# Second attention: the output projection's bias as a product of a row of ones on the matmul engine, in place of Pool's addition to the residual

## The chip, the cores and the metric

The kernel runs on one core of a Trainium2 chip. The metric is the device time of one execution in microseconds (us), and lower is better. The engines have short names here as in the profile: PE is TensorE (matrix products; PEld is its weight load), DVE is VectorE, ACT is ScalarE, POOL (or Pool) is GpSimd, SP is SyncE, which only issues DMAs. Each runs its own instruction stream; they meet at semaphores.

## The reference, cut to what matters

Eight sequences of 256 tokens, 256 features wide, go through a small tower:

```python
h = tok(x)                                   # smoothing over time, projection
h = h + attn0(layernorm(h))                  # causal softmax attention, 16 heads
h = h + moe(layernorm(h))                    # 8 experts, 2 chosen for each token
h = h + attn1(layernorm(h))                  # second attention, below
h = h + fp8_linear(layernorm(h))

# attn1, for x = its own layer norm of the input:
q, k, v = x @ Wq.T + bq, x @ Wk.T + bk, x @ Wv.T + bv      # 16 heads of 16
s = q @ k.T / 4
s = sigmoid(s - mu) * exp(s);  s = s / s.sum(-1)
out = (s @ v) @ Wo.T + bo
```

The change concerns `bo` in the last line, a vector of 256 that is added to every token's row.

## The kernel before, in words

The order of the work on each engine is written out by hand; no scheduler moves anything. The second attention is a loop over the eight batches (one sequence of 256 tokens each), called step b = 0 to 7 here. Every engine has its own `iteration(b, ...)`, and within one step the engines work on three batches at once: step b makes the scores of batch b, the projections of batch b+1, and the back end (division, output projection, residual sum, moments) of batch b-1.

PE's order in step b (the last nested functions of the kernel): the first scores `pass1(0)` to `pass1(7)`, two heads each, into two alternating PSUM areas, with other work between them: the turned input of batch b+1, the last two groups of value products of batch b-1 (`weigh_values`), `project_rows` for q and k of batch b+1 (L2045), the turns of batch b-1's result, and the output projection of batch b-1 as two token tiles, `project_token_tile(misc[0], n_oT, 3, 0)` before `pass1(7)` and `(..., 3, 1)` after it (L2051). The second tile raises `n_wo`. Then come `pass2(0)`, the value projection of batch b+1 (L2051 again), `pass2(1)` to `pass2(7)` with fillers (`idle_product`, L2081) among them, and the first two groups of value products of batch b (L2074). The scores are L2060. `pass1` and `pass2` make the same scores twice, because ACT turns one copy into exp (L845) and the other into a sigmoid (L846), changing its function table once in each step. A score pass p waits until ACT has emptied its area, pass p-2.

DVE's order in step b: division of batch b-1's result (L1550, L1558), the parts of q and k of batch b+1 (L1335, L1342), `sum_h3(b-1)` (L1568: `h` = projected rows in PSUM + `h`), its moments, `biased_v(b+1)` (L1376), then eight multiplications of the exp part by the sigmoid part (L1346), which the value products of PE wait for, two multiplications each.

Pool's order in an iteration: `gather(b+2)` (four indirect DMAs that fetch the experts' rows, L703), `biased_h(b)` (L712: h = h + bo1, both token tiles in one 128x512 instruction), two small norm steps (L690, L692), and the second bfloat16 part of q and of k for batch b+1 (L718). Pool runs ahead of PE: its iteration 0 starts before PE's step 0 has ended its first scores, and from iteration 2 on its gather and `biased_h` stand in the time of PE's step b-1.

SP copies the q and k parts into the stacked layout that the scores read (L568, twelve DMAs for each batch). `pass1(0)` of the next step waits for them to land.

`bo1` is loaded once, spread over all 128 partitions; `ones_row` is a [1, 128] row of ones that Pool fills at the start and that nothing reads. The last batch's back end stands behind the loop: two token tiles into two banks (L2308), then for each the sum with `h` (L1673) and its moments on DVE.

Of the kernel before, what the change touches and what calls it, by code (L numbers as in the profile page):

```python
# [28 lines left out]
ALU = mybir.AluOpType  # L29
# [3 lines left out]
P = 128  # L33
B, C_IN, T = 8, 128, 256
D, HEADS = 256, 16
DH = D // HEADS
QT = T // P
TILES = B * QT
TOKENS = TILES * P
DC = D // P  # L40
# [38 lines left out]
def stages(batch, first, last):  # L79

    return not isinstance(batch, int) or first <= batch <= last
# [17 lines left out]
def tower_kernel(nc, a, out):  # L99
    with ExitStack() as ctx:  # L100
        def sb(name, shape, dt):
            return ctx.enter_context(nc.sbuf_tensor(name, shape, dt))

        def sem(name):
            return ctx.enter_context(nc.semaphore(name))


        h = sb("h", [P, TILES, D], F32)
# [6 lines left out]
        w1T = sb("w1T", [P, 4, DC, D], F32)  # L115
# [5 lines left out]
        bo1 = sb("bo1", [P, D], F32)  # L121
# [3 lines left out]
        ones_row = sb("ones_row", [1, P], F32)  # L125
# [52 lines left out]
        def carve(shape, dt, size):  # L178
            n = size
            for s in shape:  # L180
                n *= s
            start = used[0]
            used[0] = start + (n + 31) // 32 * 32
            assert used[0] <= ARENA, used[0]
            v = arena[:, start:start + n].bitcast(dt)
            if len(shape) == 2:
                v = v.rearrange("p (a b) -> p a b", a=shape[0])
            if len(shape) == 3:
                v = v.rearrange("p (a b c) -> p a b c", a=shape[0], b=shape[1])
            if len(shape) == 4:  # L190
                v = v.rearrange("p (a b c d) -> p a b c d", a=shape[0], b=shape[1], c=shape[2])
            return v
# [52 lines left out]
        n_xh = carve([QT, D], F32, 4)  # L245
# [21 lines left out]
        n_oT = w0T[:, TOPK + 1]  # L267
# [34 lines left out]
        last_rows_bank = [misc[0], psum[:, 3, :]]  # L302
# [39 lines left out]
        S = {n: sem(n) for n in names}  # L342
# [3 lines left out]
        LAST = B - 1  # L346
# [115 lines left out]
        with nc.Block() as block:  # L462
# [158 lines left out]
            def _(pool):  # L621
# [38 lines left out]
                def iteration(b, u, k):  # L660
                    if stages(b - 1, 0, LAST):

                        if isinstance(b, int) and b == 1:
                            pool.wait_ge(S["w_in"], LATE_LOADS)
                        pool.wait_ge(S["xh_done"], QT * b)
                        v = h[:, bass.ds((b - 1) * QT, QT), :]
                        pool.tensor_tensor(v, v, bo0[:].rearrange("p (o d) -> p o d", o=1).to_broadcast([P, QT, D]),
                                           ALU.add).then_inc(S["hbo_done"], 1)
                    if stages(b - 1, 0, LAST):
                        norm_scale(b - 1, 1, S["mv2"], S["veps2"], S["rstd2"])  # L670
                    if stages(b + 2, 0, LAST):
                        norm_scale(b + 2, 0, S["mv1"], S["veps1"], S["rstd1"])
                    if stages(b - 2, 0, LAST):

                        pool.wait_ge(S["xslot_done"], b)
                        settled(pool)
                        for c in range(TOPK):
                            for q in range(QT):
                                pool.indirect_dma_start(  # L679
                                    out=xg, out_offset=bass.IndirectOffsetOnAxis(ap=xslot[:, c, q:q + 1], axis=0),  # L680
                                    in_=x2h[:, u, q, :], in_offset=None).then_inc(scat[u], 16)

                batches(pool, iteration, B + 2)

                def scale1(b, n, got, s_eps, s_rstd):
                    pool.wait_ge(got, QT * (b + 1))
                    settled(pool)

                    scale, shift = (1.0 + LN1_EPS, LN_EPS * LN1_EPS) if n == 0 else (1.0, LN_EPS)
                    pool.tensor_scalar(n_veps[:, n, :], n_mom[:, n, :, 1], scale, shift, ALU.mult, ALU.add).then_inc(s_eps, 1)  # L690
                    pool.wait_ge(s_eps, b + 1)
                    pool.tensor_tensor(n_rs[:, n, :], n_veps[:, n, :], half_exp[:], ALU.pow).then_inc(s_rstd, 1)  # L692

                def gather(b):

                    done = min(EARLY_TILES + 2 * EXPERTS, MOE_TILES) if b == 0 else min(2 * EXPERTS * (b + 1), MOE_TILES)
                    pool.wait_ge(S["place_step"], PLACE_STEPS)
                    for u in range(2):
                        pool.wait_ge(y_st[u], 16 * ((done + 1 - u) // 2))
                    wait(pool, S["comb_done"], 4 * b)  # L700
                    for c in range(TOPK):
                        for q in range(QT):
                            pool.indirect_dma_start(  # L703
                                out=n_y[:, c, q, :], out_offset=None, in_=yg[0:done * P, :],
                                in_offset=bass.IndirectOffsetOnAxis(ap=pos[:, c, b * QT + q:b * QT + q + 1], axis=0)
                            ).then_inc(y_in[b % 2], 16)

                def biased_h(b):

                    pool.wait_ge(S["n_xh"], QT * (b + 1))  # L710
                    v = h[:, bass.ds(b * QT, QT), :]
                    pool.tensor_tensor(v, v, bo1[:].rearrange("p (o d) -> p o d", o=1).to_broadcast([P, QT, D]),  # L712
                                       ALU.add).then_inc(S["n_hbo"], 1)

                def second_part(b, which, got, done):

                    pool.wait_ge(got, b + 1)
                    pool.tensor_copy(n_qkp[which][:, 1], n_qkr[which]).then_inc(done, 1)  # L718

                def iteration(b, u, k):  # L720
                    if stages(b + 2, 3, LAST):
                        gather(b + 2)
                    if stages(b, 0, LAST):
                        biased_h(b)
                    if stages(b - 2, 0, LAST):
                        scale1(b - 2, 1, S["m_mv"], S["m_eps"], S["m_rstd"])
                    if stages(b + 2, 3, LAST):
                        scale1(b + 2, 0, S["n_mv"], S["n_eps"], S["n_rstd"])
                    if stages(b + 1, 1, LAST):
                        second_part(b + 1, 0, S["n_qr"], S["n_qm"])  # L730
                        second_part(b + 1, 1, S["n_kr"], S["n_km"])
                    if b == 0:
                        scale1(2, 0, S["n_mv"], S["n_eps"], S["n_rstd"])

                for b in range(2):
                    gather(b)
                    scale1(b, 0, S["n_mv"], S["n_eps"], S["n_rstd"])
                gather(2)
                all_batches(iteration)

            @block.scalar
# [272 lines left out]
            def _(dve):  # L1014
# [548 lines left out]
                def sum_h3(b):  # L1563

                    dve.wait_ge(S["n_wo"], b + 1)
                    dve.wait_ge(S["n_hbo"], b + 1)
                    hv = h[:, bass.ds(b * QT, QT), :]
                    dve.tensor_tensor(hv, misc[0].rearrange("p (q d) -> p q d", q=QT), hv, ALU.add).then_inc(S["n_h3"], 1)  # L1568

# [95 lines left out]
                for q in range(QT):  # L1665
                    divided_slots(q, EARLY_SLOTS, HEADS, o1_last).then_inc(S["n_on"], 1)
                maximum(LAST - 1)
                dve.wait_ge(S["n_hbo"], B)
                dve.wait_ge(S["x3_done"], QT * LAST)
                for q in range(QT):  # L1670
                    n = LAST * QT + q
# [69 lines left out]
            def _(pe):  # L1741
# [3 lines left out]
                for j in range(DC):  # L1745
                    mm = pe.transpose(misc[0][:, j * P:(j + 1) * P], wraw[:, 8, j, 0:P], ident[:])
# [302 lines left out]
                def project_token_tile(bank, x, w, q):  # L2049
                    for c in range(DC):  # L2050
                        mm = pe.matmul(bank[:, q * D:(q + 1) * D], x[:, c, q * P:(q + 1) * P], w1T[:, w, c, :],  # L2051
                                       start=(c == 0), stop=(c == DC - 1))
                    return mm

                def scores(b, u, p, done):
# [214 lines left out]
                def kept_busy(n):  # L2270

                    for _ in range(n):
                        pe.matmul(misc[1].rearrange("p (c t) -> p c t", c=DC), identb[:], fqT[:], start=True, stop=True)
# [25 lines left out]
                for q in range(QT):  # L2299
                    pe.wait_ge(S["n_on"], QT * LAST + q + 1)  # L2300
                    for c in range(DC):
                        mm = pe.transpose(last_rows_bank[q][:, c * P:(c + 1) * P], n_onat[:, q, c * P:(c + 1) * P], ident[:])
                    mm.then_inc(S["n_ot2"], 1)
                kept_busy(1)
                for q in range(QT):
                    pe.wait_ge(S["n_oT"], B + q)
                    for c in range(DC):
                        mm = pe.matmul(last_rows_bank[q][:, 0:D], n_oT[:, c, q * P:(q + 1) * P], w1T[:, 3, c, :],  # L2308
                                       start=(c == 0), stop=(c == DC - 1))
                    mm.then_inc(S["n_wo"], 1)  # L2310
                kept_busy(8)

                pe.wait_ge(S["q_step"], 1)
# [66 lines left out]
```

## Time and profile before

| | |
|---|---|
| time, median of 3 runs | 770.08 us (767.87 to 770.21) |
| profiled execution, its own time | 775.55 us |
| its span, first to last instruction | 773.7 us |
| PE busy / DVE / ACT / POOL, share of the span | 91% / 57% / 45% / 19% |
| second attention, step 0 to the last batch's back end | about 544 us to 742 us |
| start of `pass1(0)` on PE, steps 1 to 7 | 566.4, 592.0, 615.7, 639.9, 663.8, 686.4, 709.2 us |

Times inside the profile count from the first instruction. The chain of waits is the work that ended last, followed back: each piece is what the next one waited for. "issue" in it is time in which nothing that the profile shows was waited for. An entry such as `[0.49 <-DVE arena L1346]` at the end of a row says how long the engine stood idle before it and what ended that. A float32 matmul of this kernel appears as two records, so the two matmuls of one token tile read x4. `arena` is one large buffer that holds most tiles, and `psum` all accumulators.

### The profile page before, as it was taken

The numbers are of one execution on the slowest core, as the hardware profiler recorded it, in microseconds if no ns is written. First come the engines' busy times: TensorE is split into PE (matmuls) and PEld (weight loads), VectorE is DVE, ScalarE is ACT, GpSimd is POOL, SyncE is SP. The second block draws the span as 40 slices with busy tenths as digits, with TensorE's granted clock in tenths as the row PEclk, the third lists the DMA queues.
The fourth block names the chain that finished last, engine by engine and source line by source line (L and its number), as shares of the span: only waits on it lengthen the run. The fifth ranks groups of instructions, "written<-read, shape, count | busy, mean of one in ns | idle before, by whom it ended". The sixth has DMA issues, their size and how long they took to land.

```text
span 773.7 us, 16147 instructions
## 1 busy us (share of the span) xinstructions
PE 701.8 (91%) x5671; PEld 576.0 (74%) x5681; DVE 444.4 (57%) x1129; ACT 350.6 (45%) x599; POOL 147.4 (19%) x180
## 2 busy tenths in 40 slices
PE   5697999999889999999999999999889999999855
PEld 4476777777767998999999999998556666665533
DVE  3567587778763542244322232233479988977686
ACT  2242453355335221212211212131779898899735
POOL 2010112331322021000000100200465553411000
PEclk9799999999998999999999999999999999999975
DMA  6979264466374566555555555574555774555002
GB/s 166 201 138 271 41 91 89 76 89 89 76 171 159 183 195 239 196 184 197 161 187 198 188 187 198 173 184 115 93 88 73 110 107 67 81 63 69 1 14 96
DMA packets 70839, 102.54 MB, mean 133 GB/s; under 512 B 8416, under 2 KB 58600, under 8 KB 70640
## 3 DMA queue, kind: packets, MB, share of 16 engines
q1 hardware_dynamic: 67376, 93.15, 50.4%
q0 software_dynamic: 3136, 8.40, 4.3%
q8 instruction: 43, 0.70, 0.4%
q14 instruction: 28, 0.23, 0.1%
q10 hardware_dynamic: 256, 0.07, 0.0%
HBM read 63.75 MB, written 12.58 MB: 99 GB/s over the span
## 4 chain that ended last, share of the span: by engine, by line
PE 65%; DVE 12%; DMA 8%; issue 5%; ACT 4%; POOL 2%; SPq 2%; ACTq 0%; DVEq 0%; POOLq 0%
PE psum L2102 18%; PE psum L2153 17%; DMA arena<-arena 7%; PE psum L2060 3%; PE psum L1782 3%; PE psum L2045 3%; PE psum L2074 3%; DVE arena L1346 2%; DVE arena L1199 2%; PE psum L1806 2%; POOL w0T L703 2%; PE psum L2051 1%; SPq L568 1%; PE psum L1811 1%; PE psum L2130 1%
## 5 line engine op out<-in xcount | busy, mean ns | idle before, releaser
L2102 PEld LDWEIGHTS psum<-arena 128*128 128x128 f32 x1248 | 144.9, 192 | 3.3 <-issue 1.7
L2102 PE MATMUL psum<-arena 128*128 128x128 f32 x1248 | 146.1, 275 | 1.2 <-issue 1.1
L2153 PE MATMUL psum<-arena 128*128 x624 | 141.3, 380 | 0.8 <-DVE arena L1492 0.8
L875 ACT ACTIVATE arena<-psum,arena 128x128 f32<-128x128 f32 x156 | 44.5, 368 | 190.1 <-PE psum L2102 106.6
L2153 PEld LDWEIGHTS psum<-arena 128*128 128x128 f32 x624 | 115.6, 190 | 15.3 <-issue 1.2
L1474 DVE TENSOR_SCALAR arena<-psum,arena 128x128 f32<-128x128 f32 x156 | 44.0, 344 | 81.0 <-PE psum L2102 64.8
L2060 PE MATMUL psum<-arena 96*128 96x256 bf16 x512 | 74.8, 276 | 8.4 <-ACT arena L845 4.2
L1346 DVE TENSOR_TENSOR arena<-arena 128x1024 f32<-128x1024 f32 x64 | 77.9, 1284 | 1.3 <-ACT arena L845 1.3
L1199 DVE TENSOR_REDUCE arena<-psum 128x6 f32<-128x768 f32 x64 | 59.3, 954 | 28.9 <-PE psum L1811 27.5
L703 POOL DMA_INDIRECT w0T<-yg,pos x32 | 40.3, 1260 | 185.6 <-DMA yg<-arena 177.4
L2060 PEld LDWEIGHTS psum<-arena 96*128 96x128 bf16 x512 | 44.8, 98 | 40.5 <-issue 14.7
L1492 DVE TENSOR_TENSOR arena<-psum,arena 128x256 f32<-128x256 f32 x39 | 16.6, 424 | 97.0 <-PE psum L2153 97.0
L846 ACT ACTIVATE arena<-psum,neg_mu 128x1024 f32<-128x1024 f32 x64 | 67.9, 1120 | 5.9 <-PE psum L2060 5.6
L845 ACT ACTIVATE arena<-psum 128x1024 f32<-128x1024 f32 x64 | 62.1, 1034 | 15.5 <-DVE arena L1492 7.9
L817 ACT ACTIVATE arena<-psum 128x768 f32<-128x768 f32 x64 | 48.5, 808 | 21.7 <-PE psum L1828 21.3
L1806 PE MATMUL psum<-arena 96*128 96x256 bf16 x128 | 36.8, 288 | 11.1 <-DMA arena<-arena 5.9
L679 POOL DMA_INDIRECT xg<-arena,xslot x32 | 31.5, 985 | 53.9 <-DVE xslot L1118 46.6
L1823 PE MATMUL psum<-arena 97*128 97x256 bf16 x128 | 35.9, 281 | 4.7 <-DMA arena<-arena 4.0
L656 POOL TENSOR_SCALAR veps<-mv 128x2 f32<-128x2 f32 x16 | 5.4, 339 | 173.7 <-DVE mv L1054 173.7
L2074 PE MATMUL psum<-arena 128*32 128x256 f32 x512 | 34.3, 385 | 2.6 <-DVE arena L1346 1.4
L690 POOL TENSOR_SCALAR arena<-arena 128x2 f32<-128x2 f32 x16 | 6.5, 405 | 143.0 <-DVE arena L1329 125.3
L1790 PE MATMUL psum<-w0T,arena 128*128 128x256 f32 x128 | 31.7, 401 | 2.2 <-DVE arena L1040 1.7
(309 smaller groups left out, 1201.4 us busy)
## 6 DMA issues: line engine op xcount, KB each, us to landing
arena<-in_L_ffn_w_dram SPq DMA_DIRECT2D x47, 1024.0 KB
arena<-arena SPq DMA_DIRECT2D x192, 128.0 KB, 4.6
arena<-xg SPq DMA_DIRECT2D x39, 128.0 KB
yg<-arena SPq DMA_DIRECT2D x39, 128.0 KB, 1.7
out_dram<-arena SPq DMA_DIRECT2D x8, 256.0 KB, 2.1
xg<-zeros SPq DMA_DIRECT2D x9, 128.0 KB, 2.6
arena<-in_x_dram SPq DMA_DIRECT2D x8, 128.0 KB, 3.2
arena<-in_L_ffn_b_dram SPq DMA_DIRECT2D x1, 1024.0 KB
```

The costliest lines, as they stand in the source:

```text
L703: pool.indirect_dma_start(out=n_y[:, c, q, :], out_offset=None, in_=yg[0:done * P, :], in_offset=bass.IndirectOffsetOnAxis(ap=pos[:, c, b ...
L817: act.activation(probs[:, p], area[p % 2][:, :, 0:3 * P], ACT.Exp).then_inc(S["exp_done"], 1)
L845: return act.activation(out, in_, ACT.Exp)
L846: return act.activation(out, in_, ACT.Sigmoid, bias=neg_mu[:])
L875: ins = act.activation(hidT[:, v, c, :], psum[:, 2 * v, c * P:(c + 1) * P], ACT.Relu, bias=b1c[:, v, c:c + 1])
L1199: dve.tensor_reduce(mx[:, 2 * p:2 * p + 2, :], area[p % 2][:, :, 0:3 * P].rearrange("p i (n k) -> p i n k", k=P), AX, ALU.max).then_inc(S[ ...
L1346: dve.tensor_tensor(first[:, u, p], first[:, u, p], second[:, p % 4], ALU.mult).then_inc(S["prodD"], 1)
L1806: pe.matmul(dst[:, 0:T], stackq[0:ROWS, u, hd, P:T], stackk[0:ROWS, u, hd, :], start=True, stop=False)
L2060: mm = pe.matmul(area[p % 2][:, i, kt * T:(kt + 1) * T], stackk1[u][0:ROWS, hd, kt * P:(kt + 1) * P], stackq1[u][0:ROWS, hd, :], start=Tru ...
L2074: mm = pe.matmul(pv_out[32 * i:32 * i + 32, g], n_vaug[:, u, kt, head_of(4 * g + i), :], first[:, u, 2 * g + i // 2, i % 2, kt * T:(kt + 1 ...
L2102: mm = pe.matmul(psum[:, 2 * v + c // HALF, (c % HALF) * P:(c % HALF + 1) * P], w1b[:, i % W1_BUFS, d, c * P:(c + 1) * P], xtT[:, v, d, :] ...
L2153: mm = pe.matmul(y_bank, hidT[:, u, c, :], w2s[:, one(e), c, :].rearrange("p o n -> p (o n)"), start=(c == 0), stop=(c == HC - 1))
```

## The change: what it does

Pool's `biased_h` goes, with its wait for `n_xh` and with DVE's two kinds of waits for `n_hbo` (in `sum_h3` and in the last batch). On PE each token tile of the output projection gets a third product into the same accumulator: `ones_row` as the stationary operand (one row, 128 columns), `bo1[0:1]` as the moving one (one row, 256 columns), both float32. There are 16 such products, two for each batch. Nothing else is edited; the other operands, buffers and waits stay.

```diff
-                def biased_h(b):
-
-                    pool.wait_ge(S["n_xh"], QT * (b + 1))
-                    v = h[:, bass.ds(b * QT, QT), :]
-                    pool.tensor_tensor(v, v, bo1[:].rearrange("p (o d) -> p o d", o=1).to_broadcast([P, QT, D]),
-                                       ALU.add).then_inc(S["n_hbo"], 1)
...
-                    if stages(b, 0, LAST):
-                        biased_h(b)
...
                 def sum_h3(b):
                     dve.wait_ge(S["n_wo"], b + 1)
-                    dve.wait_ge(S["n_hbo"], b + 1)
...
                 maximum(LAST - 1)
-                dve.wait_ge(S["n_hbo"], B)
...
                 def project_token_tile(bank, x, w, q):
                     for c in range(DC):
                         mm = pe.matmul(bank[:, q * D:(q + 1) * D], x[:, c, q * P:(q + 1) * P], w1T[:, w, c, :],
-                                       start=(c == 0), stop=(c == DC - 1))
+                                       start=(c == 0), stop=(c == DC - 1 and w != 3))
+                    if w == 3:
+                        mm = pe.matmul(bank[:, q * D:(q + 1) * D], ones_row[:], bo1[0:1, :], start=False, stop=True)
                     return mm
...
-                        mm = pe.matmul(last_rows_bank[q][:, 0:D], n_oT[:, c, q * P:(q + 1) * P], w1T[:, 3, c, :],
-                                       start=(c == 0), stop=(c == DC - 1))
-                    mm.then_inc(S["n_wo"], 1)
+                        pe.matmul(last_rows_bank[q][:, 0:D], n_oT[:, c, q * P:(q + 1) * P], w1T[:, 3, c, :],
+                                  start=(c == 0), stop=False)
+                    pe.matmul(last_rows_bank[q][:, 0:D], ones_row[:], bo1[0:1, :], start=False, stop=True
+                              ).then_inc(S["n_wo"], 1)
```

PE in step 1, around the output projection, before (the scores are L2060, the two token tiles `w1T,w0T`, the value projection `w1T,arena`):

```order
L2060 MATMUL psum<-arena 128x256 x8
L2051 MATMUL psum<-w1T,w0T 128x256 x2
L2060 MATMUL psum<-arena 128x256 x4
L2051 MATMUL psum<-w1T,w0T 128x256 x2
L2060 MATMUL psum<-arena 128x256 x4
L2051 MATMUL psum<-w1T,arena 128x256 x4
L2060 MATMUL psum<-arena 128x256 x8
```

The same place of PE after the change, where the lines have moved up by 9 to 11:

```order
L2051 MATMUL psum<-arena 128x256 x8
L2040 MATMUL psum<-w1T,w0T 128x256 x2
L2043 MATMUL psum<-bo,ones_row 128x256
L2051 MATMUL psum<-arena 128x256 x4
L2040 MATMUL psum<-w1T,w0T 128x256 x2
L2043 MATMUL psum<-bo,ones_row 128x256
L2051 MATMUL psum<-arena 128x256 x4
L2040 MATMUL psum<-w1T,arena 128x256 x4
L2051 MATMUL psum<-arena 128x256 x8
```

One product stands ahead of the last first-pass scores and one ahead of the first second-pass scores; the value projection and all later passes stand behind both.

Pool at the start of the loop, before (gather of batch 2, addition for batch 0, parts of q and k of batch 1, norm steps, gather of batch 3, addition for batch 1):

```order
L703 DMA w0T<-yg,pos 128x256 x4
L712 TENSOR_TENSOR h<-h,bo 128x512
L718 CAST arena<-arena 128x512 x2
L690 TENSOR_SCALAR arena<-arena 128x2
L692 TENSOR_TENSOR arena<-arena,half_exp 128x2
L703 DMA w0T<-yg,pos 128x256 x4
L712 TENSOR_TENSOR h<-h,bo 128x512
L690 TENSOR_SCALAR arena<-arena 128x2
```

The same place of Pool after the change:

```order
L703 DMA w0T<-yg,pos 128x256 x4
L711 CAST arena<-arena 128x512 x2
L690 TENSOR_SCALAR arena<-arena 128x2
L692 TENSOR_TENSOR arena<-arena,half_exp 128x2
L703 DMA w0T<-yg,pos 128x256 x4
L690 TENSOR_SCALAR arena<-arena 128x2
```

The parts of q and k now follow the gather directly in iteration 0; from iteration 1 on the norm steps do.

## Rows read from the trace of the kernel before

**Rows 1.** Chain of waits in step 4: start, length, what ran.

```profile
650.74 1.13 PE psum L2051 x4
651.87 0.44 PE psum L2060 x4
652.31 0.86 PE psum L2051 x4
...
653.62 1.74 PE psum L2051 x8
...
656.07 5.63 DVE arena L1346 x4
...
662.91 0.85 issue
```

**Rows 2.** Token tiles of the output projection: ns min/median/max, weight load and matmul.

```profile
L2051 PEld LDWEIGHTS psum<-w1T,w0T x56: 186/190/193, 579.8 to 720.2; 128*128 128x128 f32 x56
L2051 PE MATMUL psum<-w1T,w0T x56: 377/379/484, 579.8 to 720.4; 128*128 128x256 f32 x56
```

**Rows 3.** Pool's eight additions, in the same columns.

```profile
L712 POOL TENSOR_TENSOR h<-h,bo x8: 1265/1370/1432, 551.8 to 698.3; 128x512 f32<-128x512 f32 x8
```

**Rows 4.** Timeline of DVE: the eight multiplications of steps 4 and 6.

```profile
655.99 10.24 DVE L1346 TENSOR_TENSOR arena<-arena 128x1024 f32<-128x1024 f32 x8
...
702.53 9.16 DVE L1346 TENSOR_TENSOR arena<-arena 128x1024 f32<-128x1024 f32 x8
```

**Rows 5.** Timeline of Pool beside the multiplications of step 4.

```profile
658.04 1.43 POOL L712 TENSOR_TENSOR h<-h,bo 128x512 f32<-128x512 f32 x1
```

**Rows 6.** Timeline of DVE in step 0: the rest of q.

```profile
551.32 0.88 DVE L1335 SCALAR_TENSOR_TENSOR arena<-psum,cols,arena 128x256 f32<-128x256 f32 x2 [6.15 <-ACT arena L853]
```

**Rows 7.** Chain of waits from step 0 to step 1.

```profile
551.83 1.28 POOL h L712
553.10 0.56 POOL arena L718
...
564.92 5.67 POOL w0T L703
...
573.63 1.68 DVE h L1356 x4
```

**Rows 8.** Timeline of PE: groups of steps 1 to 4 with idle time ahead.

```profile
578.49 0.63 PE L2039 MATMUL psum<-ident,w0T 128*128 128x128 f32 x4 [2.54 <-DVE arena L1335]
...
590.99 1.07 PE L2074 MATMUL psum<-arena 128*32 128x256 f32 x16 [0.49 <-DVE arena L1346]
...
614.07 1.07 PE L2074 MATMUL psum<-arena 128*32 128x256 f32 x16 [0.22 <-DVE arena L1346]
615.69 0.60 PE L2060 MATMUL psum<-arena 96*128 96x256 bf16 x4 [0.55 <-issue]
...
639.92 0.60 PE L2060 MATMUL psum<-arena 96*128 96x256 bf16 x4 [1.13 <-issue]
...
663.76 0.60 PE L2060 MATMUL psum<-arena 96*128 96x256 bf16 x4 [0.85 <-issue]
```

**Rows 9.** Timeline of the weight loads: ahead of step 3's first scores.

```profile
615.66 0.35 PEld L2060 LDWEIGHTS psum<-arena 96*128 96x128 bf16 x4 [1.01 <-DMA arena<-arena]
```

**Rows 10.** Chain of waits: ends of steps 5 and 6, step 7, behind the loop.

```profile
686.29 0.08 issue
...
709.09 0.09 issue
...
719.99 0.16 issue
...
737.82 1.14 PE psum L2308 x4
```

**Rows 11.** Timeline of DVE: the last batch's two sums.

```profile
739.10 0.42 DVE L1673 TENSOR_TENSOR h<-psum,h 128x256 f32<-128x256 f32 x1 [1.43 <-PE psum L2308]
...
740.12 0.39 DVE L1673 TENSOR_TENSOR h<-psum,h 128x256 f32<-128x256 f32 x1
```

## The prediction

> **What bounds the kernel now.** I read the page's busy shares first, then the chain of waits over the second attention, then each engine's timeline at the places the change touches. The shares say that Pool is idle four fifths of the time and PE almost never, so the change moves work from the idlest engine to the busiest; whether that costs anything is read from the waits of each step.
>
> In steps 1 to 6 the chain runs through the very place that is edited: first token tile, scores, second tile, scores, value projection, all on PE, then DVE's multiplications, then PE's value products and the next step's first scores [rows 1]. Two things in that chain matter. PE still idles ahead of the value products or of the next first scores in steps 1 to 4 [rows 8]: in step 1 for DVE's multiplications (0.49 us), in step 2 for them (0.22) and then for the stacked q and k to land (0.55), in steps 3 and 4 mainly for the landing (1.13 and 0.85). That it is the landing is told by the weight load there, whose wait a DMA ended [rows 9]. That DMA path starts at the q and k projections, which stand ahead of the token tiles in PE's order, so a longer token tile does not delay it. Steps 5 and 6, where nothing is gathered any more, leave PE only 0.08 and 0.09 us at that point [rows 10].
>
> **The change part by part.**
>
> *Added: 16 products on PE.* A token tile's four records take 0.86 us in the chain, the value projection's eight take 1.74 [rows 1], so one record costs 0.217 us and one float32 product with 256 columns, two records, 0.435; a batch's pair costs 0.87. The new product has the same columns and type, but one row in place of 128; no row of this trace has that. From below, four bfloat16 score products with as many columns take 0.44 [rows 1], 0.11 each; from above, a tile that follows a wait takes 1.13 [rows 1], 0.565 per product. I take 0.435, the row with the same type and columns.
>
> The weight load of a record, 0.19 us [rows 2], lies beside the record before it: four records of 0.379 us, each with its own load, leave 0.86 in the chain [rows 1], so loads add nothing to the term. The Trainium skill, "TensorE: Matmul & The Clock Gate", Part 3 ("The mechanism"), says the contrary for a case like this: a weight load overlaps running products only when it goes to another row group. Full-height tiles here do hide their loads, so the trace disagrees for them; no run here shows it for a one-row operand behind a full one. By that rule the sum below would be +7.7 us; it is the fourth rival.
>
> Where the pair lands: the last first-pass scores come 0.435 later, all second-pass scores but the first 0.87, and with them ACT, which works from what PE gives it. The value projection ends 0.87 later, so the multiplications begin 0.87 later. The cost of a step is 0.87 less the idle time of PE before the next first scores: step 1: 0.87 - 0.49 = 0.38; step 2: 0.87 - 0.22 - 0.55 = 0.10; step 3: none, 1.13 covers it; step 4: 0.87 - 0.85 = 0.02; step 5: 0.87 - 0.08 = 0.79; step 6: 0.87 - 0.09 = 0.78 [rows 8, 10]. In step 7 no values are projected, and what counts is when ACT gets its last first-pass scores, one product late: 0.435 - 0.16 of slack [rows 10] = 0.28. Behind the loop both tiles are on the path: the first ends at 737.82 + 1.14 = 738.96 [rows 10], its sum starts 0.14 later; the second would be ready at 738.96 + 0.87 + 0.14 = 739.97, while its sum starts at 740.12 [rows 11]. With 0.87 more it is 740.84: 0.72 late. Together 3.07 us.
>
> *Removed: eight additions on Pool, 1.37 us each* [rows 3]. Pool's time is worth nothing in itself; two effects are. First, in steps 1 to 4 an addition runs beside the multiplications [rows 5], and the eight of step 4 take 10.24 us against 9.16 in step 6, where no addition is beside them [rows 4]: 1.08 us, and it falls on one of the first four, which take 5.63 [rows 1]. When the additions go, the multiplications start 0.87 late and the fourth ends 0.21 early. So this buys no time by itself: it keeps DVE from holding up the value products, and the idle time above can absorb PE's delay. Between no relief and all of it, I take all; with none, step 1 would lose all 0.87 and step 2 0.87 - 0.55 = 0.32, 0.7 us more.
>
> Second, in step 0 one addition is on the chain: Pool does it before the second part of q [rows 7]. The rest of q is ready at 551.32 + 0.88 = 552.20 [rows 6]; the copy follows the addition at 553.10 [rows 7]. It can start about 0.1 us after 552.20, so 0.8 earlier. Behind it on Pool stand k's part, the norm steps and the next gather; all of that is the chain down to the sum at 573.63 [rows 7] and PE's turn at 578.49, ahead of which PE idles 2.54 us [rows 8]. So the 0.8 arrives: -0.8. The other additions (start of step 1, steps 5 and 6) have no one waiting behind them.
>
> *Waits.* None is added. DVE's wait for the addition goes, but the addition was done long before the projected rows it is summed with. The next thing late is always PE.
>
> *The sum:* +3.07 - 0.8 = +2.27 us. The profiled execution took 775.55 us (span 773.7 and 1.85 around it), so 777.8 under the profiler; it stands 5.5 us above the median of the runs, and I carry the difference over to that median: 770.08 + 2.27 = 772.35. With the bounds of the product, by the same subtraction: at 0.11, steps 1 to 4 and 7 lose nothing, 5 and 6 lose 0.14 and 0.13, the end 0.07, so 0.34 - 0.8 = -0.5 us; at 0.565, 0.64 + 0.36 + 0 + 0.28 + 1.05 + 1.04 + 0.41 + 0.98 - 0.8 = +4.0 us.
>
> **The rivals.**
>
> *Clearly slower: the landing is no cover.* The runs are 5.5 us shorter than the profiled execution; if part of this is that the stacks land earlier there, steps 2 to 4 wait only for DVE (0.22 in step 2 [rows 8], taken for all three) and lose 0.65 each, 1.95 in place of 0.12: +4.1 us, 774.2. For it speaks that the cover is thin (0.55 and 0.85 against 0.87); against it that 1.01 us of a weight load's wait is a DMA's [rows 9], and DMA time is the least likely to shrink unprofiled. It decides from the point at which the landing comes 0.5 us earlier.
>
> *No change: the long descriptor run goes.* One indirect DMA in step 0 takes 5.67 us on Pool [rows 7], beside five multiplications back to back. If the shifted phases let it through earlier, step 0 gains as much as PE idles behind it, 2.54 [rows 8], not 0.8: +0.5 us, 770.6. Against it: Pool and DVE move together there, so their phases stay.
>
> *Slightly faster: one-row products are nearly free*, at the lower bound: -0.5 us, 769.6. Nothing in the rows speaks for it but the bfloat16 pace.
>
> *Much slower: each record of a product exposes its weight load*, 0.19 us [rows 2]: 0.815 for a product, 1.63 for a pair. Step by step 1.14 + 0.86 + 0.50 + 0.78 + 1.55 + 1.54 + 0.66 + 1.48 - 0.8 = +7.7 us, 777.8. The hidden loads of the full tiles speak against it [rows 1, 2]. It is what the rule of the Trainium skill quoted above would do here.
>
> **How the numbers follow.** Main case 0.50; no cover 0.27; long run gone 0.13; nearly free 0.06; exposed loads 0.04. A measurement of this kernel tells about 0.3% from no change, 2.3 us. The main case, 772.4 with its own range 771.2 to 773.4, sits on that line: 0.24 of its 0.50 is within, 0.25 above, 0.01 below. No cover and exposed loads are slower (0.30, and 0.01 within); the long run gone is within (0.12, and 0.01 below); nearly free is within for 0.04, below for 0.02. That makes faster 0.04, same 0.41, slower 0.55. The range 769.7 to 775.2 holds the main case, no cover with a microsecond above it and the long run gone; left out are the exposed loads and half of the nearly free case, and the runs' own scatter.
>
> **What would show it.** Right: two new records per product, 0.21 to 0.22 us apart; token tiles of 1.3 us in the chain; no addition on Pool and every set of eight multiplications near 9.2 us; step 0's copy of q's part at about 552.25 on the same clock; the first scores of steps 1 to 7 moved by about -0.8, -0.4, -0.3, -0.3, -0.3, +0.5 and +1.3 us; the last batch's second sum 0.7 late against its first tile's start. Wrong: if steps 3 to 5 grow too, the landing was no cover; if the total moves by less than 1 us, step 0 gave more than its 0.8; if multiplications still show a long one, something else of Pool holds DVE up.

## The result, and the profile after

The changed kernel took 776.09 us (median of 6 runs, 774.64 to 777.96) against 769.35 us for the kernel before beside it (6 runs, 766.81 to 770.21): ratio 1.0072 (95% interval [1.0043, 1.0101]), or 5.5 us; the medians alone stand 6.7 us apart. Twelve later runs gave 776.64 us against 771.22 us, 1.0077 [1.0044, 1.0110], or 5.9 us (medians 5.4 us apart). Ratios, here and below, are of the fast runs alone and leave out two slow ones, 1019.66 us with the additions moved and 791.77 us with two products. So it is slower, as forecast, but by more than twice the 2.27 us of the sum, and above the range.

The two profiled spans, 773.7 and 776.1 us, differ by only 2.4 us. That is because in the profile after, the first scores of step 0 stand at 539.50 us, before at 543.79, and nothing ahead of step 0 was edited. From there to the end it is 229.95 us before and 236.64 after, 6.7 us longer. The loop has therefore to be read step by step. The table has the time from each step's first scores to the next (step 7: to the end of the span), from the PE timelines. A star marks a step in which the granted clock fell below 0.75 for some 3 to 4 us ahead of the last batch's back end. The last 27 to 30 us of every one of these kernels run at 0.50 and carry no star: from the last batch's second sum to the end each takes 33.6 to 33.7 us.

| kernel | steps 0+1 | 2 | 3 | 4 | 5 | 6 | 7 and behind |
|---|---|---|---|---|---|---|---|
| before | 48.20 | 23.70 | 24.23 | 23.84 | 22.61 | 22.81 | 64.56* |
| changed | 49.53* | 24.11 | 24.37 | 24.10 | 23.81 | 24.12 | 66.60* |
| changed, repeated | 49.76* | 24.12 | 24.39 | 24.31 | 23.81 | 24.11 | 65.00 |
| 128 rows (full height) | 49.23* | 23.63 | 24.49 | 23.51 | 23.22 | 23.52 | 64.11 |
| 96 rows | 48.88* | 23.51 | 24.43 | 23.63 | 23.21 | 23.51 | 64.09 |
| 64 rows | 49.83* | 24.10 | 24.17 | 24.58 | 23.81 | 24.11 | 65.00 |
| 32 rows | 48.20 | 24.11 | 24.14 | 24.23 | 23.81 | 24.11 | 65.01 |
| neither product nor addition | 46.90 | 23.49 | 24.14 | 23.88 | 22.58 | 22.73 | 64.51* |
| two products | 49.11 | 24.97 | 24.84 | 25.33 | 24.68 | 24.96 | 66.62 |
| products and additions | 49.94 | 24.65 | 24.66 | 24.66 | 23.95 | 24.11 | 66.29* |
| additions moved, no product | 47.40 | 23.34 | 24.16 | 23.66 | 22.52 | 22.63 | 64.57* |

Steps 5 and 6 repeat to 0.01 us between the two profiles of the changed kernel and those with 32 and 64 rows. They are what the causes are read from.

The chain of waits of the kernel after, in step 5, through both token tiles (start, length, what ran; the scores are L2051 now, the tiles and the value projection L2040, the new product L2043). It is the place of [rows 1] one step later:

```profile
672.45 1.13 PE psum L2040 x4
673.58 0.62 PE psum L2043 x2
674.20 0.54 PE psum L2051 x4
674.75 0.86 PE psum L2040 x4
675.61 0.62 PE psum L2043 x2
676.24 0.54 PE psum L2051 x4
676.78 1.73 PE psum L2040 x8
```

The tile keeps its 0.86 us. The product's two records take 0.62 us, not 0.435, and the four scores behind it 0.54, not the 0.44 of [rows 1]. A product thus lengthens the chain by 0.62 + 0.10 = 0.72 us, a pair by 1.44. Each start stands 0.31 or 0.32 us behind the one ahead of it at three places (first record, second record, next scores), where a tile's records stand 0.22 apart.

The timeline of the weight loads shows what is held up, at the first of these two products:

```profile
673.51 0.29 PEld L2043 LDWEIGHTS psum<-bo,ones_row 1*128 1x128 f32 x2 [0.33 <-issue]
674.13 0.33 PEld L2051 LDWEIGHTS psum<-arena 96*128 96x128 bf16 x4 [0.33 <-issue]
```

The load unit idles 0.33 us ahead of the product's loads and again ahead of the scores' loads. The first load starts only 0.31 us behind the start of the tile's last record, so the product can't start earlier. It is so at all 16 products of this trace.

The new line by itself (ns min/median/max, weight load and matmul):

```profile
L2043 PEld LDWEIGHTS psum<-bo,ones_row x28: 181/182/184, 577.1 to 723.5; 1*128 1x128 f32 x28
L2043 PE MATMUL psum<-bo,ones_row x28: 374/426/478, 577.1 to 723.7; 1*128 1x256 f32 x28
```

The weight load is even a little shorter than the tiles' 190 ns [rows 2]; it comes late, it isn't longer. Half of the matmul records last 478 ns instead of 374: the first of each product.

DVE's multiplications in the kernel after, in step 4 and step 5, the rows that answer to [rows 4], and all 64 together:

```profile
655.04 9.16 DVE L1337 TENSOR_TENSOR arena<-arena 128x1024 f32<-128x1024 f32 x8
679.15 9.16 DVE L1337 TENSOR_TENSOR arena<-arena 128x1024 f32<-128x1024 f32 x8
...
L1337 DVE TENSOR_TENSOR arena<-arena x64: 1215/1219/1226, 556.2 to 734.0; 128x1024 f32<-128x1024 f32 x64
```

Step 4's set took 10.24 us before; now none of the 64 is longer than 1.226 us, where the longest was 2.300.

Step 0 in the kernel after, first DVE's rest of q, then Pool (rows that answer to [rows 6, 7]):

```profile
548.32 0.88 DVE L1326 SCALAR_TENSOR_TENSOR arena<-psum,cols,arena 128x256 f32<-128x256 f32 x2 [7.44 <-ACT arena L844]
```

```profile
546.59 0.95 POOL L703 DMA_INDIRECT w0T<-yg,pos  x1 [0.30 <-issue]
549.27 0.61 POOL L711 CAST arena<-arena 128x512 bf16<-128x512 f32 x1 [1.74 <-DVE arena L1326]
...
561.15 5.67 POOL L703 DMA_INDIRECT w0T<-yg,pos  x1 [0.30 <-issue]
```

The copy of q's part begins 0.07 us after the rest of q is done (548.32 + 0.88 = 549.20). Before, it began 0.90 us after (552.20 to 553.10). The indirect DMA of 5.67 us is still there, unchanged.

PE's idle time in the kernel after, ahead of step 4's first scores and inside step 4, which answers to [rows 8]:

```profile
637.51 0.60 PE L2051 MATMUL psum<-arena 96*128 96x256 bf16 x4 [0.49 <-DMA arena<-arena]
656.04 0.61 PE L2051 MATMUL psum<-arena 96*128 96x256 bf16 x4 [0.34 <-ACT arena L837]
```

Of the 1.13 us of waiting for the stacked q and k, 0.49 is left. Ahead of the value products PE no longer waits for DVE in steps 1 to 6.

Behind the loop, the chain of the kernel after (tiles L2299, products L2301, sum L1662), which answers to [rows 10, 11]:

```profile
738.97 1.13 PE psum L2299 x4
740.10 0.62 PE psum L2301 x2
740.73 1.06 PE psum L2299 x4
741.79 0.64 PE psum L2301 x2
742.43 0.02 issue
742.45 0.43 DVE h L1662
```

From the first tile's start to the second sum's start it is 3.48 us, where it was 740.12 - 737.82 = 2.30 [rows 10, 11]: 1.18 us more, not 0.72.

Last, what disturbs a comparison of single steps. Stretches of the kernel after around step 0: length, busy time (and count) of PE, PEld, DVE, ACT and Pool, granted clock, DMA share, GB/s:

```profile
540.00:543.00 3.00, 1.63 (x13) 1.17 (x12) 0.88 (x3) 1.96 (x3) 0.28 (x1) 1.00 0.13 44
543.00:547.00 4.00, 3.85 (x12) 2.77 (x13) 0.00 (x0) 2.83 (x5) 3.08 (x4) 0.57 0.25 69
547.00:550.00 3.00, 3.00 (x20) 2.48 (x19) 0.96 (x3) 2.21 (x5) 1.14 (x2) 1.00 0.43 116
```

The granted clock falls from 1.00 (2.4 GHz) towards the lower level (1.2 GHz; the mean of the 4 us is 0.57) after a stretch in which PE was busy 1.63 of 3 us, and returns. Step 0 lost by it what its own gain was worth and more. The kernel before has such a fall in step 7, the kernel after a second one there.

### The profile page after: what moved, and what is told of

It is laid out like the page before. It is cut to its first block, busy times and chain, and to the rows that moved or that the text cites. A ratio compares the mean times of both kernels' runs of the same rounds, so it can differ in the third digit from the quotient of the medians.

```text
span 776.1 us, 16206 instructions
## 1 busy us (share of the span) xinstructions
PE 713.6 (92%) x5713; PEld 580.8 (75%) x5713; DVE 438.4 (56%) x1129; ACT 351.5 (45%) x599; POOL 134.2 (17%) x172
## 4 chain that ended last, share of the span: by engine, by line
PE 72%; DVE 10%; DMA 7%; issue 5%; ACT 4%; POOL 1%; SPq 1%; ACTq 0%; DVEq 0%; POOLq 0%
PE psum L2093 18%; PE psum L2144 17%; DMA arena<-arena 5%; PE psum L2051 5%; PE psum L2034 3%; PE psum L2065 3%; PE psum L1771 3%; PE psum L2040 3%; DVE arena L1190 2%; PE psum L1795 2%; PE psum L1779 1%; PE psum L2121 1%; PE psum L1800 1%; PE psum L1833 1%; POOL w0T L703 1%
## 5 line engine op out<-in xcount | busy, mean ns | idle before, releaser
L2051 PE MATMUL psum<-arena 96*128 96x256 bf16 x512 | 73.8, 277 | 6.9 <-ACT arena L836 3.5
L2051 PEld LDWEIGHTS psum<-arena 96*128 96x128 bf16 x512 | 44.5, 98 | 39.2 <-issue 12.6
L1337 DVE TENSOR_TENSOR arena<-arena 128x1024 f32<-128x1024 f32 x64 | 73.4, 1219 | 0.0
L703 POOL DMA_INDIRECT w0T<-yg,pos x32 | 37.9, 1186 | 184.9 <-DMA yg<-arena 176.5
```

Source lines behind the costliest of these rows:

```text
L703: pool.indirect_dma_start(out=n_y[:, c, q, :], out_offset=None, in_=yg[0:done * P, :], in_offset=bass.IndirectOffsetOnAxis(ap=pos[:, c, b ...
L1337: dve.tensor_tensor(first[:, u, p], first[:, u, p], second[:, p % 4], ALU.mult).then_inc(S["prodD"], 1)
L2051: mm = pe.matmul(area[p % 2][:, i, kt * T:(kt + 1) * T], stackk1[u][0:ROWS, hd, kt * P:(kt + 1) * P], stackq1[u][0:ROWS, hd, :], start=Tru ...
```

## The experiments

The first question was why a pair of products costs 1.44 us. The theory: the change of height (the rows, that is partitions, of the operands), from 128 rows to one and back, leaves weight loads uncovered. The rival: any added product costs this much there. The second question was what Pool's additions had cost.

**Full height.** The product takes the identity and the bias spread over 128 partitions, which gives the same sum.

```diff
-    ... ones_row[:], bo1[0:1, :], start=False, stop=True
+    ... ident[:], bo1[:], start=False, stop=True
```

> The bias product with full-height operands: the 128x128 identity as stationary, the bias row spread over 128 partitions as moving operand; same columns, same place. Theory A (the one-row product is slow because it differs in height from its neighbours: it takes 0.63 us in the changed kernel's chain where the neighbours' pace gives 0.435, its weight load not being hidden): each product goes back to 0.43-0.44, steps 5 and 6 lose 0.8 us each in place of 1.2, the whole gains about 16 x 0.19 less what idle time covers = 2 to 3 us on the changed kernel, so 772 to 774 us, a ratio of about 1.004 to 1.006 to the kernel before. Theory B (the height does not matter; the loss is from somewhere else, such as the slow clock in step 0): same time as the changed kernel, ratio about 1.007, and a product still takes 0.63.

Measured: 775.06 us against 771.73, ratio 1.0034 [1.0008, 1.0060], or 2.6 us. The chain in step 5:

```profile
675.83 0.87 PE psum L2040 x4
676.70 0.43 PE psum L2043 x2
677.13 0.44 PE psum L2051 x4
```

With the same columns, type and number of products, the product costs 0.43 us and the scores behind it their usual 0.44. The loads run early, beside the record ahead, and the product starts on time (weight load, then product):

```profile
676.32 0.41 PEld L2043 LDWEIGHTS psum<-bo,ident 128*128 128x128 f32 x2
676.54 0.59 PE L2043 MATMUL psum<-bo,ident 128*128 128x256 f32 x2
```

The price of the prediction is the price of a full-height product, and the run's +2.6 us is near the +2.27 of its sum. Steps 5 and 6 cost 0.61 and 0.71 us over before; steps 2 to 6 together cost 1.18 us, where the prediction's terms for them add up to 1.69 and the one-row kernel has 3.32. The ratio lies a little under the expected 1.004 to 1.006, which its interval reaches. It is the height, not the added product.

**Two products.** A second one-row product, with a row of zeros, ahead of the first in each tile.

```diff
+    pe.matmul(..., ones_row[:], zeros[0:1, :], start=False, stop=False)
     mm = pe.matmul(..., ones_row[:], bo1[0:1, :], start=False, stop=True)
```

> Two one-row products per token tile, the added one with a row of zeros. Theory A1 (what costs extra is the change of height, going into and out of the one-row product): the second costs 0.435, the two together about 1.07 us, and the kernel is about 5 us slower than the changed one, near 781 us, ratio about 1.014. Theory A2 (every one-row product is slow, 0.63 each): two take 1.26, the kernel is about 8 us slower than the changed one, near 784 us, ratio about 1.018.

Measured: 783.94 us (median of 6), ratio 1.0184 [1.0140, 1.0229]. The chain in step 5 (L2043 and L2044 are the two products, L2052 the scores):

```profile
673.33 0.87 PE psum L2040 x4
674.20 0.62 PE psum L2043 x2
674.82 0.43 PE psum L2044 x2
675.25 0.54 PE psum L2052 x4
```

The second product costs 0.43 us, though it too has one row: its loads are covered. The 0.10 us at each of three places are paid once for going to one row and back, with one such product between as with two. So theory A1 holds for the price. The time of the whole run is nearer to A2's (ratio 1.018) than to A1's (1.014), but that does not speak for A2: from step 0 to the end this kernel takes 240.51 us and the one with 32 rows 233.61, neither with a fall of the clock ahead of the back end, and the 6.9 us between them are 16 times 0.43. A1's sum for the whole run was too low.

**64, 32 and 96 rows.** The same product on the first 64, 32 or 96 rows of the identity and of the spread bias, so that the bias reaches only as many tokens of a tile.

```diff
-    ... ones_row[:], bo1[0:1, :], start=False, stop=True
+    ... ident[0:64, :], bo1[0:64, :], start=False, stop=True     # 32; 96
```

> The bias product with 64 rows: the upper 64 rows of the identity and of the spread bias (the bias reaches half of the tokens). Theory A1 (a height other than its neighbours' exposes the weight load): the next group starts 0.94 us behind the tile's last record, as with one row, and steps 5 and 6 take 23.8 and 24.1 us. Rival (only a height within one row group of 32 does): 0.65 us, as with 128 rows, and 23.2 and 23.5 us.

> The same with 32 rows. Theory A1 and its rival: 0.94 us behind the tile's last record, steps 5 and 6 of 23.8 and 24.1 us. If it shows 0.65 us, the single row itself is what costs, not the height of the row group.

> The bias product on 96 rows (rows 0 to 95 of the identity by rows 0 to 95 of the spread bias, so the bias reaches 96 of 128 tokens of a tile). With 64, 32 and 1 row each product's records stood 0.31, 0.32 and 0.31 us from the record before, with 128 rows 0.22 each. If any height that differs from the token tile's exposes the weight loads: 0.31, 0.32, 0.31 again, a product of 0.72 us, steps 5 and 6 of 23.8 and 24.1 us. If only an operand that leaves half of the rows or more unused does it (the scores' bfloat16 operands of 96 rows stand 0.11 us from the float32 tiles, no more than their own pace): 0.22 throughout, a product of 0.435 us, steps 5 and 6 of 23.2 and 23.5 us as in the full-height run. The whole run is one look, 773 to 781 us either way, and tells nothing by itself.

Measured, one execution each: 780.16, 777.35 and 773.07 us. The chain in step 5, with 64 rows, with 32, and with 96:

```profile
678.56 0.86 PE psum L2040 x4
679.42 0.63 PE psum L2043 x2
680.05 0.54 PE psum L2051 x4
```

```profile
675.74 0.86 PE psum L2040 x4
676.61 0.62 PE psum L2043 x2
677.23 0.54 PE psum L2051 x4
```

```profile
673.27 0.86 PE psum L2040 x4
674.13 0.43 PE psum L2043 x2
674.57 0.44 PE psum L2051 x4
```

With 64 and 32 rows it is the one-row price, with 96 the full-height price; steps 5 and 6 agree (23.81 and 24.11; 23.81 and 24.11; 23.21 and 23.51). The three traces repeat it at every one of their 16 products: the first load starts 0.31 us behind the start of the record ahead with 64 and 32 rows (0.37 at one place, where the clock was low), and 0.002 us behind it with 96. So it is neither the single row nor any difference of height: the extra time comes with an operand of 64 rows or fewer between ones of 96 or 128 rows (float32 tiles ahead, bfloat16 scores or a float32 tile behind). Heights between 64 and 96 weren't tried, and why a load is held back there stays open.

**Neither product nor addition.** The changed kernel without its products; it leaves the bias out.

```diff
-                    if w == 3:
-                        mm = pe.matmul(..., ones_row[:], bo1[0:1, :], start=False, stop=True)
```

> Neither the products nor Pool's addition (the output projection's bias is left out). Theory A (all of the loss is the products' time on PE): faster than before by what the addition cost, 0.8 us in step 0 and up to 0.5 in step 1 and 0.2 in step 2, so 767.5 to 768.5 us, ratio 0.998 to 0.999; the eight multiplications of every step take about 9.2 us. Theory B (the loss comes from what the removal of the addition does to Pool and DVE): still slower than before, ratio 1.003 or more.

Measured: 771.29 us against 771.73, ratio 1.0003 [0.9973, 1.0033]. PE ahead of the first scores of steps 4 and 5:

```profile
635.98 0.60 PE L2049 MATMUL psum<-arena 96*128 96x256 bf16 x4 [1.61 <-DMA arena<-arena]
659.86 0.60 PE L2049 MATMUL psum<-arena 96*128 96x256 bf16 x4 [1.18 <-DMA arena<-arena]
```

Without the additions PE is earlier and waits longer for the landing (1.61 and 1.18 us against 1.13 and 0.85 [rows 8]). Steps 0 to 6 take 163.72 us against 165.39: 1.7 us gained, 1.3 of it in steps 0 and 1. The whole run does not show so little. Without the products the loss is gone, so all of it is theirs.

**Products and additions.** The products stay, and Pool's eight additions come back, with zeros in place of the bias.

```diff
+                def biased_h(b):
+                    pool.wait_ge(S["n_xh"], QT * (b + 1))
+                    v = h[:, bass.ds(b * QT, QT), :]
+                    pool.tensor_tensor(v, v, zeros[:]..., ALU.add).then_inc(S["n_hbo"], 1)
```

> The changed kernel with Pool's eight additions back in their old places, adding a tile of zeros, and DVE's waits for them. Theory A: this undoes the two gains of the removal: 0.8 us in step 0, and in steps 1, 2 and 4 the multiplications are 1.08 us longer again so that PE waits 0.2 to 0.5 us for them; about 2 us slower than the changed kernel, 777 to 778.5 us, ratio 1.009 to 1.012. Theory B (the removal brought nothing): same as the changed kernel, ratio 1.007.

Measured: 781.13 us, ratio 1.0110 [1.0072, 1.0147]. DVE's multiplications in step 4 are long again:

```profile
657.07 10.36 DVE L1346 TENSOR_TENSOR arena<-arena 128x1024 f32<-128x1024 f32 x8
```

In steps 0 to 6, where neither has a fall of the clock, this kernel takes 171.97 us and the one with 32 rows 168.60. Beside the products the additions are worth 3.4 us: 1.7 in steps 0 and 1, then 0.54, 0.52, 0.43, 0.14 and 0. That is more than the 1.7 us they are worth without the products. A likely reason, not followed wait by wait: in this kernel PE waits for the landing ahead of no step's first scores, so nothing covers its waits for a late multiplication (0.26 us in steps 3 and 4); in the kernel before, 1.13 and 0.85 us of waiting for the landing stand behind them [rows 8].

**Additions moved.** The kernel before, with Pool's additions at another place: those of batches 0 and 1 behind the second gather, those of batches 2 to 5 behind the second norm step two batches on.

```diff
-                    if stages(b, 0, LAST):
+                    if b == 1:
+                        biased_h(0)
+                    if b == 1 or LAST - 2 < b <= LAST:
                         biased_h(b)
...
+                    if 2 <= b <= LAST - 2:
+                        biased_h(b)
```

> The kernel before, with no product; Pool's additions stay but move in Pool's order: those of batches 0 and 1 behind the gather of step 1 (off the chain of step 0), those of batches 2 to 5 behind the second norm step of their iteration (Pool idles there and the multiplications are over); the last two stay. Theory A (what the addition costs is its place): it reaches what the kernel without any bias reaches, steps 0 and 1 together 1.0 to 1.3 us shorter than before, steps 2 to 6 as before, 768 to 770 us, ratio 0.997 to 0.999, and every set of eight multiplications near 9.2 us. Theory B (at the new place it holds up the division or the rest of q on DVE): steps 2 to 5 grow by up to 1 us each, ratio 1.000 to 1.004.

Measured: 771.90 us against 771.22, ratio 1.0013 [0.9985, 1.0041]. Step 4, DVE's multiplications and Pool's addition ahead of them:

```profile
647.71 9.16 DVE L1350 TENSOR_TENSOR arena<-arena 128x1024 f32<-128x1024 f32 x8
```

```profile
636.93 1.27 POOL L712 TENSOR_TENSOR h<-h,bo 128x512 f32<-128x512 f32 x1
```

The additions run where DVE multiplies nothing, and the sets of steps 1 to 6 take 9.16 or 9.17 us. Steps 0 to 6 take 163.71 us, 1.7 less than before and the same as with no additions at all; in steps 0 and 1 it is 0.8 us, less than the 1.0 to 1.3 expected. No step grew, so theory B's reason is out, though the ratio lies in its range and above that of theory A. The relief that the change bought with products is to be had in the steps by another order alone; but its 0.2% is within the interval, so this version is not shown to beat the kernel before. No other run gave a faster one.

**The changed kernel again.**

> The changed kernel once more, beside the others on one chip. Expected: ratio 1.005 to 1.010 to the kernel before; steps 5 and 6 of 23.8 and 24.1 us as in its first profile; steps 0 and 1 together 48.2 to 48.4 us where the granted clock does not fall in them (49.5 with the fall at 544 to 547 us in the first profile).

Measured: 776.64 us, 1.0077 [1.0044, 1.0110]. Steps 2 to 6 agree with the first profile to 0.21 us. The first profile had falls of the clock in steps 0 and 7; this one has one, in step 1, and its step 7 is 1.6 us shorter (length, busy times, clock as above):

```profile
572.00:575.00 3.00, 0.67 (x5) 0.64 (x6) 2.15 (x10) 0.72 (x2) 1.52 (x3) 0.94 0.79 129
575.00:578.00 3.00, 3.00 (x13) 2.19 (x11) 2.91 (x6) 2.58 (x3) 1.40 (x2) 0.50 1.14 118
```

What steps 0 and 1 take without a fall this run therefore can't show; the kernel with 32 rows shows it, 48.20 us.

## Why the prediction was wrong in size, point by point

| term | predicted, us | measured, us |
|---|---|---|
| one product | 0.435 | 0.72 |
| steps 0 and 1 (-0.8 + 0.38) | -0.42 | 0.00 (with 32 rows, no fall in either) |
| step 2 | +0.10 | +0.41 |
| step 3 | 0 | +0.14 |
| step 4 | +0.02 | +0.26 |
| step 5 | +0.79 | +1.20 |
| step 6 | +0.78 | +1.31 |
| step 7 and behind | +1.00 | about +1.7 to +2.0, estimated |
| sum | +2.27 | about +5.0 to +5.3; timed +5.5 and +5.9 |

The estimate for step 7: the kernel before has a fall of the clock there, and in the changed kernel a fall there cost 66.60 - 65.00 = 1.6 us. Without one, before would take about 64.56 - 1.6 = 63.0, the changed kernel takes 65.0. In the kernel with products and additions, whose fall comes at nearly the same place of step 7 as in the kernel before, it cost 66.29 - 65.00 = 1.3 us; by that it is 63.3 and +1.7. Of this, 1.18 us were measured directly, behind the loop.

**The step that failed** is the price: "I take 0.435, the row with the same type and columns", and with it "so loads add nothing to the term". The full-height run shows that the arithmetic behind the price was right for a full-height operand. The one-row product adds 0.29 us to it, 0.10 at its first record, at its second and at the next scores, because its load and that of the scores behind it are not started beside the record ahead. The hidden loads of the full-height tiles [rows 1, 2] said nothing about a load of one row behind them. The upper bound of 0.565, taken from a tile that follows a wait, did not hold this either; the sum at that bound was +4.0 us, and so the top of the range lay too low.

With 1.44 for a pair in its own subtraction the prediction gives 0.15 for steps 0 and 1, then 0.67, 0.31, 0.59, 1.36, 1.35, and 0.56 + 1.29 behind: +6.3 us, 1.0 to 1.3 above the sum of the table. So the subtraction was nearly right. One part of the rest is idle time that it left out: ahead of the value products PE waits for DVE in steps 3 and 4 of the kernel before too (timeline of PE):

```profile
637.72 1.07 PE L2074 MATMUL psum<-arena 128*32 128x256 f32 x16 [0.49 <-DVE arena L1346]
661.84 1.07 PE L2074 MATMUL psum<-arena 128*32 128x256 f32 x16 [0.22 <-DVE arena L1346]
```

The relief that covers PE's delay in steps 1 and 2 covers it there as well. At the price of 0.435 this changes next to nothing, since the landing alone covers steps 3 and 4. At 1.44 a pair it takes step 3 from 0.31 to 0 and step 4 from 0.59 to 0.37, and the sum to +5.8 us. Another part is that idle time printed by the profile is short by about 0.07 us a wait here: the starts of the records have 0.48 us ahead of the next first scores in step 6 before and 0.32 after, so 0.16 of idle time, where the chain's "issue" had 0.09; in step 4 it is 1.23 - 0.31 = 0.92 for 0.85. What is left was not traced further.

**Exposed loads, the rival with 0.04,** was nearest in the price of a product (0.815 us) and right that loads come into the open; its +7.7 us lies about as far above the time as the +4.1 us of the rival without cover lies below it, and that one has the wrong cause. It was wrong on which: not each record's 0.19 us, but about 0.10 at three places. The rule beside it, in the Trainium skill, "TensorE: Matmul & The Clock Gate", Part 3 ("The mechanism"), lets a load run beside a product only in another row group; the same section also lets one be pulled ahead that goes to the background weight buffer. The first of these alone the trace does not bear out: two one-row products share their rows, and the second one's loads are covered (0.43 us). Whether the second is at work no run here shows.

**Step 0** came as predicted: the copy follows the rest of q 0.07 us behind its end, where it was 0.90, so 0.83 earlier. PE's turns in step 1, to which the chain through Pool leads, stand 578.49 - 543.79 = 34.70 us behind step 0's first scores in the kernel before and 33.92 with 32 rows, where no fall of the clock disturbs it: 0.78 us. What was off in steps 0 and 1 is the pair of products behind those turns.

**The multiplications** came as predicted too, 9.16 or 9.17 us in each set of steps 1 to 7; step 0's took 9.81 before and after. Taking all of the relief was right.

**The landing** was cover: step 4's first scores still wait 0.49 us for it, step 3 grew by 0.14, and the rival without cover falls, as far as a profiled execution can tell. The prediction names growth of steps 3 to 5 as a sign against the cover. In step 4 it follows from the price, since a pair at 1.44 is more than the idle time there, 0.22 + 0.85 us; the 0.14 us of step 3, whose 0.49 + 1.13 us would hold the pair, were not traced. **The long descriptor run** did not go (5.67 us), and **nearly free** falls with the price.

**The baseline** held: carrying the difference over to the median was right, since the timed difference and that of the undisturbed steps agree.

## What to carry to other kernels

Price a new product by the operands beside it, not only by its columns and type: here a bias row of one partition behind a full-height float32 tile cost 0.72 us, the same sum with 128 rows 0.43, and a product of 96 rows no more. Work taken off an idle engine gains only what others wait for: without the products, eight additions of 1.37 us were worth 1.7 us, and moving them away from DVE's multiplications gave as much in the steps. And compare steps between two profiles, not spans: here the spans differed by 2.4 us, the edited part by 6.7, of which some 1.5 are one more fall of the clock.

## What the runs showed of the hardware that was not expected

- A float32 product on 1, 32 or 64 rows between ones of 96 or 128 rows costs about 0.10 us at its first record, its second and the next product behind it, as its weight load starts 0.31 us behind the start of the record ahead in place of 0.002. One of 96 or 128 rows costs nothing extra, and a second one-row product behind a one-row product nothing either.
- A short fall of the granted clock (to 0.50, over some 3 to 4 us) comes at a varying place of the loop: in steps 0 and 7 of one execution of the changed kernel, in step 1 of the next, nowhere in the loop with 32 rows or with two products. The two shown above follow a stretch in which PE was busy for 1.63 or 0.67 of 3 us. Where it falls on the path it costs 1.3 to 1.6 us, about as much as the pair of products.
